# Attention rows: four engines' programs written out for 240 blocks instead of a loop of eight

## What is computed

```python
mod_k = K[src] + 0.2 * rel[:, None, :]
scores = jnp.einsum('ehd,ehd->eh', Q[dst], mod_k) / D ** 0.5
seg_max = jax.ops.segment_max(scores, dst, num_segments=N)
ex = jnp.exp(scores - seg_max[dst])
denom = jax.ops.segment_sum(ex, dst, num_segments=N)
agg = jax.ops.segment_sum(w[:, :, None] * V[src], dst, num_segments=N)
```

## Time and profile before

| | us |
|---|---|
| median of 3 runs | 6525.7 |
| range of the runs | 6525.26 to 6539.23 |
| the profiled execution, its own time | 6547.7 |
| its span in the profile | 6545.9 |
| mean granted TensorE clock | 0.825 of full |

### The profile page before, as it was taken

One profiled execution on the slowest core, in us unless ns is written; L12 is line 12 of the kernel. 1 busy time (PEld: TensorE's weight loads), 2 busy tenths in 40 slices (PEclk: granted clock), 3 DMA queues, 4 the chain that ended last, 5 costly groups with the idle time before them and its releaser, 6 DMA issues. The chain is left out here.

```text
span 6545.9 us, 78959 instructions
## 1 busy us (share of the span) xinstructions
PE 4536.7 (69%) x20233; PEld 3162.5 (48%) x20234; DVE 3510.2 (54%) x7039; ACT 1794.2 (27%) x5528; POOL 3319.3 (51%) x2377
## 2 busy tenths in 40 slices
PE   3778797796775555555655637623991699998978
PEld 3456565574553344444444423321561477776446
DVE  8575754745517566666666656660114444443245
ACT  0222332322221444545444420000220112221122
POOL 0011786885877555556655557656555344441000
PEclk9889899898888676777777668656996899998989
DMA  6998313213224655655555224324992455553000
GB/s 230 310 361 287 71 2 70 30 2 81 15 13 105 172 172 164 169 163 162 159 147 160 47 52 124 96 53 155 307 296 68 147 200 200 200 200 137 1 24 20
DMA packets 775999, 879.34 MB, mean 134 GB/s; under 512 B 392349, under 2 KB 645312, under 8 KB 771496
## 3 DMA queue, kind: packets, MB, share of 16 engines
q1 hardware_dynamic: 348392, 633.65, 28.4%
q0 software_dynamic: 417328, 235.13, 17.6%
q10 hardware_dynamic: 10128, 8.79, 0.4%
HBM read 682.29 MB, written 240.09 MB: 141 GB/s over the span
## 5 line engine op out<-in xcount | busy, mean ns | idle before, releaser
L741 POOL DMA_INDIRECT pairs<-REC,FARC x800 | 1665.9, 2082 | 969.0 <-DMA pairs<-REC,FARC 482.4
L1021 PE MATMUL a_pa<-a_VW,identf 128*128 128x260 f32 x1920 | 734.1, 537 | 130.9 <-issue 123.3
L919 POOL DMA_INDIRECT a_KV<-kv_tab,KEYS x600 | 601.0, 1002 | 387.2 <-ACT a_VW L983 210.3
L1021 PEld LDWEIGHTS a_pa<-a_VW,identf 128*128 128x128 f32 x1920 | 487.6, 267 | 264.6 <-issue 150.0
L1009 PE MATMUL a_pq<-QS,a_ohT 128*128 x720 | 168.3, 359 | 595.2 <-issue 316.7
L919 POOL DMA_INDIRECT XN<-kv_tab,KEYS x360 | 366.9, 1019 | 279.0 <-ACT a_VW L983 172.2
L983 ACT ACTIVATE a_VW<-a_KV,a_VW 128x64 f32<-128x64 f32 x1800 | 446.2, 335 | 4.9
L2289 DVE TENSOR_TENSOR AIN<-AIN,w_pin 128x512 f32<-128x512 f32 (+1 forms) x325 | 216.5, 666 | 429.7 <-PE w_pin L2328 424.6
L1009 PEld LDWEIGHTS a_pq<-QS,a_ohT 128*128 128x128 bf16 x720 | 78.9, 110 | 716.9 <-issue 696.0
L1706 PE MATMUL m_bank<-m_QK,m_VX 128*128 128x320 f32 x1280 | 360.5, 441 | 3.6 <-ACT m_QK L1596 3.6
L1697 PE MATMUL m_bank<-m_VX,m_QK 128*128 128x256 f32 x1600 | 352.1, 381 | 2.5 <-ACT m_QK L1602 2.5
(11 more groups left out here) (566 smaller groups left out, 9367.2 us busy)
## 6 DMA issues: line engine op xcount, KB each, us to landing
pairs<-ZERO SPq DMA_DIRECT2D x32, 5000.0 KB, 39.6
e_W<-in_L_ffn_w SPq DMA_DIRECT2D x192, 512.0 KB
REC<-pairs SPq DMA_DIRECT2D x100, 800.0 KB, 6.1
RES<-pairs SPq DMA_DIRECT2D x13, 3200.0 KB, 10.1
HB<-pairs SPq DMA_DIRECT2D x12, 3200.0 KB, 10.3
m_crow<-cell_tab SPq DMA_DIRECT2D x75, 488.3 KB
row_tab<-a_arow SPq DMA_DIRECT2D x240, 130.0 KB
n_AR<-row_tab SPq DMA_DIRECT2D x30, 1040.0 KB, 5.2
```

What stands on the lines that cost most here:

```text
L741: pool.indirect_dma_start(self.pairs[half], bass.IndirectOffsetOnAxis(self.FARC[:, i:i + 1].bitcast(I32), 0), self.REC[:, i, 0:4].bitcast( ...
L919: pool.indirect_dma_start(KV[t % UB][:, j, :], None, self.kv_tab, bass.IndirectOffsetOnAxis(self.SIDX[:, t * ROW + j:t * ROW + j + 1], 0), ...
L1021: last = pe.matmul(sums[b], self.identf[:, :], VW[:, b, e, :, :], start=e == 0, stop=e == ROW - 1)
```

## The change

`steps` gets a guard so that it makes no empty loop, and four calls of it, in `att_rows` only, ask for RB // UB = 30 peeled groups. All 240 blocks of SyncE, VectorE, ScalarE and TensorE are then written out. The step functions, the buffers, the order of the work and all semaphore values stay as they were; GpSimd's program is not touched.

```diff
     for u in range(peel * unroll):
         step(u // unroll, u % unroll)
-    with eng.Fori(peel, count // unroll) as i:
-        for u in range(unroll):
-            step(i, u)
+    if peel < count // unroll:
+        with eng.Fori(peel, count // unroll) as i:
+            for u in range(unroll):
+                step(i, u)
...
-                    steps(sp, RB, UB, 10, step, 2)
+                    steps(sp, RB, UB, 10, step, RB // UB)
...
-                    steps(dve, RB, UB, 2, step)
+                    steps(dve, RB, UB, 2, step, RB // UB)
...
-                    steps(act, RB, UB, 4, step)
+                    steps(act, RB, UB, 4, step, RB // UB)
...
-                    steps(pe, RB, UB, 3, step)
+                    steps(pe, RB, UB, 3, step, RB // UB)
```

## The result

The changed kernel takes 6469.2 us (median of 4 runs, 6456.1 to 6474.7) beside 6532.5 us of the kernel before in the same comparison (4 runs, 6525.3 to 6545.1). The ratio is 0.990, with a 95% interval of 0.987 to 0.992, so the gain is 63 us. The forecast was 26 us, a time of 6500. The direction was right, the size was less than half of what came. The guard in `steps` adds a line, so line 952 of before is 953 here and so on.

A forecast was written before the change was run, and what follows sets the result against it. The prediction took the stage to be bound by waits. VectorE's 56 us removed less 12 us of fetches made 44, of which 0.6, 26 us, would arrive: 6525.7 - 26 = 6500 us, range 6440 to 6560, likeliest case 6482 to 6512.

The forecast's parts named there:

- The bound: Attention-row loop: no engine is full, waits bound it; an uninterrupted run of gathers seems to hold TensorE's signal to VectorE back.
- VectorE resumed 2.0 us after GpSimd had stopped: At VectorE's wait before line 952: the release comes 2.0 us after GpSimd's gathers stop, read at two places.
- Removed, terms 1 and 2: VectorE in the loop: address arithmetic before lines 964 and 966, 24 and 20 us, and the loop's branch, 12 us.
- Removed, term 3: Register instructions and branches of ScalarE, TensorE and SyncE: costed at nothing, TensorE's branches worth 12 us at most.
- Added: Code fetches for 232 more written-out blocks: VectorE's 33 packets taken at 12 us, TensorE's 59 at 0.
- The share of 0.6: Part of VectorE's 44 us that reaches the end, the rest being lost just before long waits: 26 us.
- A: Rival: the long waits also become rarer, one in seven gone, 52 us more, about 6450 us; chance 0.17.
- B: Rival: GpSimd's cycle of gathers and waits sets the stage, so nothing moves, 6526 us; chance 0.21.
- C: Rival: GpSimd's short stops vanish and holds of VectorE lengthen, 6537 to 6584 us, middle 6560; chance 0.19.
- D: Rival: written-out code itself is slow, 11.1 us a block against 7.22 in the loop, 905 us more; chance 0.02.
- The rule on branches: VectorE's loop branch: by the skill's rule a fetch for each of 29 passes, 51 us instead of 12, giving 6477 us.

The follow-up runs named there:

- the broken run: Changed kernel with GpSimd waiting, before every second block's gathers, until the last block's gathers have landed: 6557.1 us, 1.0024 of the kernel before.
- the clean pair: Kernel before with two gathers a block instead of four, 6124.5 us, and the changed kernel with the same two gathers, 6073.0 us.
- set 3: On one chip, beside the kernel before at 6559.1 us: whole change 6528.0 us, all but VectorE's part 6576.9, all but SyncE's 6575.4.

## Why the prediction was right in direction and wrong in size

**The bound.** "So the stage is bound by waits" holds where the kernel before takes over 6500 us. The reading that TensorE's signal is held back by an uninterrupted run of gathers is supported twice: half of the gathers on such a chip leave 10.7 us of long waits, and the broken run leaves VectorE 4.6 us of waits that the profile names "remote", beside 65.1 us that it can't name.

What is late is the signal, not TensorE's work. The relation matmuls of the block that VectorE waits for until 2502.03 had ended at 2491.68 + 0.82 = 2492.50 us, 9.5 us before (TensorE in the kernel before, timeline):

```profile
2491.68 0.82 PE L1012 MATMUL a_pr<-a_rel,a_otT 64*128 64x64 bf16 x12
```

The single matmuls of the earlier trace rows belong to later work. Taking the blocks of both engines in order, 61 of VectorE's 65 waits over 2 us at this line end within 0.2 us of an update of TensorE's semaphore, and the matmul that sends it had ended 6.3 to 26.1 us earlier (median 9.6); in the changed kernel it is 46 of 48, with a median of 10.1 us, and with the broken run none of 101.

The number beside it, argued from two places, "VectorE resumed 2.0 us after GpSimd had stopped", is no law. The changed kernel has places like it, in TensorE's timeline and in GpSimd's: a gather ends at 2517.45 + 1.00 = 2518.45 us, TensorE goes on at full rate from 2518.47, VectorE resumes 1.5 us later, at 2519.93.

```profile
2515.65 0.22 PE L1013 MATMUL a_pr<-a_rel,a_otT 64*128 64x64 bf16 x1 [1.23 <-issue]
2517.06 0.26 PE L1013 MATMUL a_pr<-a_rel,a_otT 64*128 64x64 bf16 x2 [1.19 <-issue]
2518.47 3.62 PE L1022 MATMUL a_pa<-a_VW,identf 128*128 128x260 f32 x8 [1.15 <-issue]
```

```profile
2517.45 1.00 POOL L920 DMA_INDIRECT a_KV<-kv_tab,KEYS  x1 [0.30 <-issue]
2524.32 0.99 POOL L920 DMA_INDIRECT a_KV<-kv_tab,KEYS  x1 [5.88 <-ACT a_VW L984]
```

VectorE at the end of this wait:

```profile
2519.93 1.22 DVE L953 TENSOR_TENSOR a_t<-a_KV,a_pr 128x1024 f32<-128x1024 f32 x1 [6.34 <-remote]
```

But counted over the whole stage, 15 of 72 waits of VectorE over 2 us end in the kernel before while gathers run on without a stop, and 26 of 80 in the changed one.

**Removed, terms 1 and 2.** Predicted 56 us; the small gaps fell by 54.3 us in the first comparison and by 53.8 us in the clean pair. Right.

**Removed, term 3.** ScalarE's, TensorE's and SyncE's register work at nothing: SyncE alone and ScalarE alone gave 0.9998 and 0.9999, TensorE alone 1.0002 and all three together 0.9999 or 1.0020. Right as a direct cost. Where there are long waits they do shift them, SyncE's by 47 us in set 3, which the forecast left out.

**Added.** VectorE's fetches were taken at 12 us. The "issue" parts in the groups of after are 0.9 + 1.2 + 1.2 + 0.6 us on the lines shown, and in the clean pair the other lines' idle time rose by 2.4 us: it is a few us. The count was about right, 75 packets on that queue (above 80 expected), and TensorE's 46 of 16 KB (59 expected) cost nothing that shows. The net saving was thus 51.5 us where the forecast had 44. Put at nothing without a word was that the time in which VectorE is busy would fall too, by 8 us in the first comparison and 13 in the clean pair; why it does wasn't tested.

**The share of 0.6 is the step that failed.** It held that a saving just before a long wait is lost, and that the waits themselves stay as they are. Neither is a property of the kernel. The share is about 1.0 where VectorE is the bound (51.5 of 51.4 us), and about 0.2 where GpSimd is (11 us, for all but SyncE's part; the whole change wasn't run there). With long waits there is no fixed share: the saving is made, and the long waits, 400 to 500 us in all, settle at another sum. In the first comparison's profiles they fell by 23.5 us, which with the net saving of 51.5 (54.3 less 2.8) makes 75 us. Since those two executions lie 17 us further apart than the medians, little of the 23.5 need be left at the medians: the 63 us are the whole net saving, 51.5, and some 12 us of fewer long waits or busy time that can't be parted (the interval of the gain runs from 51 to 82 us). On two other chips the whole change was worth 31 and 36 us, and VectorE's part alone, on one, 6 us with an interval that holds no change.

**The rivals.** A, long waits rarer, took part in the first comparison: GpSimd's waits fell by 64 us, VectorE's long waits by 23.5. Its mechanism, a quicker VectorE that gets more blocks through between them, is not borne out: with VectorE written out they stand anywhere from 408 to 512 us. B is nearly what happens where there are no long waits (11 us with VectorE's part, none without it). C, longer holds, didn't come to the whole change, but the version without SyncE's part is its mild form: 511.9 us of long waits and 1.0021. D was excluded by the first profile. The forecast had said that it would be wrong if the stage fell by more than 60 us; it fell by 83.

**The rule on branches.** The Trainium skill, "Runtime: NRT & Kernel Launch", section "Instruction fetch mechanics", has a branch stall for a fetch when its target lies outside the two pages held, and gives 256 instructions to a block of 16 KiB. The forecast's "By the rule it would be a fetch for each of 29 passes" left that condition out: a pass of VectorE's loop is 143 instructions in the trace, so by the page its target is still held. The trace agrees: 19 packets in 1675 us are fewer than the passes, and in the clean pair the gap before the one-hot line, "issue" 11.9 us in 28 pieces, 0.42 each, went down to 0.6 us. The 6477 us that the forecast took from the rule were nearer to the time than 6500, but not for its reason.

What stays open is how GpSimd's gathers hold TensorE's signals back and whether by their rate or their bytes, why it shows in three sets and the first comparison and not in two sets, whether that is the chip or the time, and what sets the sum of the long waits from one version to the next. That a chip with long waits still has them at three gathers a block, or at half the bytes, wasn't seen, since those runs fell on a chip without them.

## What to carry to other kernels

Address arithmetic from a register cost VectorE 0.1 us for each operation that follows a drain, and a loop's branch 0.42 us; written out, both are gone and the code's fetches cost almost nothing, but the time comes back only where that engine is the bound, which is to be tested by easing the others (here two gathers instead of four). When waits that no engine's work explains fill a quarter of a stage, treat them as a quantity that any edit can move either way, and judge the edit on several chips. To tell a late signal from late work, compare the end of the instruction that sends it with the start of the one that waits: here 9.5 us lay between them. The large gain lies there: where they are absent the kernel before takes some 360 us less, nearly six times what the change brought.

## What the runs showed of the hardware

- The same program takes 6538 to 6566 us on three chips (6532 in the first comparison) and 6168 and 6170 us on two, and the difference lies in the one stage that gathers without a pause: its blocks take 7.2 us on the former, 5.6 us on the latter (each from one profile), with gathers 1.30 us apart on both. Repeated runs within a set don't change sides (25 runs from 6519 to 6559, 31 from 6157 to 6178). The DMA engines are busier on the latter (0.69 with SyncE written out against 0.58 in the kernel before, from 2157 to 3400 us), so a high load on them is not by itself what makes the waits.
- On the former a semaphore update of TensorE reaches VectorE 6 to 26 us after the matmul that sends it has ended, at the 61 waits counted above. On the latter, in the kernel with SyncE written out, 235 of the 239 recorded updates of that semaphore come within 0.1 us of such a matmul's end; in the kernel before of the first comparison 45 of 236 do.
- In the place shown on the former, TensorE's short matmuls come singly, with 1.2 us of idling before each, while gathers are issued one behind the other, and they go on together 0.02 us after a gather's end. Half of the gathers ends the long waits, and a pause after every eight leaves VectorE few that are for late signals.
- A wait of GpSimd for its own last gathers to land costs 359 / 93 = 3.9 us on average.
